# A patch transformer layer with top-1 experts: a per-image root moved from GpSimd to ScalarE, gate logits one reduction later, a chunk's loads reordered

## The reference

```
h    = patches @ W.T + b + pos                      # (32, 1024, 64)
p    = softmax((h@Wq.T+bq) @ (h@Wk.T+bk).T / 8)     # with a mask where q or k starts with 0
h    = norm(h + (p @ (h@Wv.T+bv)) @ Wo.T + bo)
e    = argmax(h @ gate_w + gate_b)                  # 8 experts, probability prb = softmax(...)[e]
pos  = place of the token in its expert's queue; kept = pos < 5120
y    = relu(h @ w1[e] + b1[e]) @ w2[e] + b2[e]      # for kept tokens
h    = norm(h + nan_to_num(y * prb * kept))
norm(x) = (x - mean(x)) / sqrt(var(x) + 1e-5)
```

## Time and profile before

| | |
|---|---|
| median of 3 runs | 1057.18 us (1056.9 to 1058.4) |
| the profiled execution | 1059.39 us, its span in the trace 1057.6 us |
| TensorE's mean granted clock | 0.952 of full speed |
| busy, of the span | TensorE 90%, VectorE 80%, ScalarE 66%, GpSimd 65% |
| windows 8 to 29 | 28.27 and 28.7 us in turn |
| from the last score window's start to the end | 892.5 to 1057.6 us |

### The profile page before, as it was taken

One profiled execution on the slowest core, in us unless ns is written; L12 is line 12 of the kernel. 1 busy time (PEld: TensorE's weight loads), 2 busy tenths in 40 slices (PEclk: granted clock), 3 DMA queues, 4 the chain that ended last, 5 costly groups with the idle time before them and its releaser, 6 DMA issues.

```text
span 1057.6 us, 19702 instructions
## 1 busy us (share of the span) xinstructions
PE 952.4 (90%) x6046; PEld 530.8 (50%) x6046; DVE 846.5 (80%) x1709; ACT 697.7 (66%) x1192; POOL 691.5 (65%) x689
## 2 busy tenths in 40 slices
PE   3799999999999999999999999999999999856740
PEld 2355545555555555555555555555555555433420
DVE  3667787788888888899989988888889897575561
ACT  2355655777777777777777777777777766545650
POOL 0015444456777777777777777777777777777775
PEclk9699999999999999999999999999999999967775
DMA  3332224334435243334443343424343333035300
GB/s 91 81 77 58 58 59 112 99 85 105 106 79 130 75 110 103 94 96 108 103 107 96 104 109 93 121 68 121 94 104 97 97 93 103 21 106 145 103 22 10
DMA packets 72503, 96.25 MB, mean 91 GB/s; under 512 B 15923, under 2 KB 52230, under 8 KB 72398
## 3 DMA queue, kind: packets, MB, share of 16 engines
q1 hardware_dynamic: 55566, 77.87, 29.7%
q0 software_dynamic: 16832, 17.11, 5.4%
HBM read 43.68 MB, written 18.11 MB: 58 GB/s over the span
## 4 chain that ended last, share of the span: by engine, by line
PE 57%; DVE 23%; ACT 9%; issue 7%; DMA 2%; POOL 1%; SPq 1%; POOLq 0%; DVEq 0%; ACTq 0%
PE p_u L590 14%; DVE mx L1003 8%; PE p_st L568 7%; PE p_misc L605 6%; PE p_misc L513 6%; PE p_misc L669 5%; PE p_misc L536 4%; PE p_sm L550 3%; ACT uu L793 3%; PE p_misc L653 3%; DVE qk L988 2%; ACT qk L759 2%; PE p_st L572 2%; PE p_sm L669 2%; ACT b_h L835 2%
## 5 line engine op out<-in xcount | busy, mean ns | idle before, releaser
L1376 POOL DMA_INDIRECT out<-b_o,b_ix x270 | 295.4, 1094 | 93.4 <-issue 69.3
L1363 POOL DMA_INDIRECT slots<-rows,idx x256 | 252.2, 985 | 146.8 <-issue 87.0
L1003 DVE TENSOR_REDUCE mx<-p_sm 128x1 f32<-128x1024 f32 x252 | 307.1, 1218 | 38.6 <-PE p_sm L552 35.6
L788 ACT ACTIVATE pT<-p_st 128x1024 f32<-128x1024 f32 x256 | 261.8, 1023 | 93.4 <-PE p_st L574 80.5
L590 PE MATMUL p_u<-pT,vv 128*64 128x512 f32 x1024 | 253.7, 605 | 0.0
L568 PE MATMUL p_st<-hi,hx 64*128 64x512 f32 x256 | 127.3, 497 | 5.1 <-ACT pT L788 4.0
L570 PE MATMUL p_st<-hx,hi 64*128 64x512 f32 x256 | 127.3, 497 | 0.0
L590 PEld LDWEIGHTS p_u<-pT,vv 128*64 128x64 f32 x1024 | 61.5, 136 | 105.2 <-issue 94.9
L550 PE MATMUL p_sm<-kh,hi 64*128 64x512 f32 x252 | 103.1, 409 | 10.3 <-DVE mx L1003 6.7
L568 PEld LDWEIGHTS p_st<-hi,hx 64*128 64x128 f32 x256 | 46.9, 183 | 127.3 <-issue 99.7
L835 ACT ACTIVATE b_h<-p_misc,b_w 128x256 f32<-128x256 f32 x244 | 95.6, 475 | 11.5 <-PE p_misc L653 5.2
(11 more groups left out here) (194 smaller groups left out, 1908.5 us busy)
## 6 DMA issues: line engine op xcount, KB each, us to landing
b_w<-in_w SPq DMA_DIRECT2D x136, 193.5 KB
hx<-hi SPq DMA_DIRECT2D x64, 256.0 KB, 3.6
b_in<-slots SPq DMA_DIRECT2D x136, 66.0 KB
lx<-lo SPq DMA_DIRECT2D x32, 256.0 KB
xt<-in_x SPq DMA_DIRECT2D x32, 196.0 KB
out<-b_o,b_ix POOLq DMA_INDIRECT x270
kh<-kh SPq DMA_DIRECT2D x32, 128.0 KB, 2.2
lx<-lo SPq DMA_DIRECT2D x32, 128.0 KB
```

Source lines behind the costliest of these rows:

```text
L788: act.activation(pT[k % 4][:, :], flat(p_st), ACT.Exp).then_inc(exp_done, 1)
L1003: dve.tensor_reduce(mx[:, p, at:at + 1], flat(max_place(n, j)), AX.X, ALU.max).then_inc(max_done, 1)
L1363: pool.indirect_dma_start(slots, bass.IndirectOffsetOnAxis(ap=idx[:, p, j:j + 1], axis=0), rows[:, p, j, :], None, bounds_check=SLOTS - 1, ...
L1376: pool.indirect_dma_start(out_rows, bass.IndirectOffsetOnAxis(ap=b_ix[:, o, j:j + 1], axis=0), b_o[:, o, j, :], None, bounds_check=T - 1, ...
```

## The change

Four edits:

- The root of the norm behind the attention is made on ScalarE for every image (`norm_root`: logarithm into sd, exponent into rstd), at place 5, or at place 6 in windows with a chunk. The two GpSimd steps and tile ve are gone. `norm_rows` on GpSimd and `gate_logits` on VectorE wait for the same semaphore as before, rstd_ready.
- `gate_logits` moves to place 6 in windows with a chunk, behind `row_max` of that place.
- HIK goes from 2 to 1, and the call of `qk_high` from ahead of the place's exponent to the end of the place.
- `load_chunk` asks for a chunk's rows first, then its four weights; inside the windows each weight waits for one more score of the window (places 4 to 7).

```
-HIK = 2
+HIK = 1
...
-        PS = 2
+        PS = 1
...
                     sp.dma_start(b_in[:, r, u, t, :], unit_rows(at[k])).then_inc(c_loaded[r], 16)
-
+                for k in range(2 * PAIRS):
+                    v, u = k // 2, k % 2
+                    if c < INSIDE:
+
+                        sp.wait_ge(st_done, NT * (HOST[c] - 1) + NT // 2 + 1 + k)
                     sp.dma_start(b_w[:, r, v, u, :], w[bass.ds(e[k], 1), :, :].rearrange("a k f -> (a k) f"))\
                         .then_inc(c_loaded[r], 16)
...
-            def last_deviation():
-                act.wait_ge(vs_ready, NB)
-                act.activation(sd[:, :], vs[:, :], ACT.Ln, bias=b_eps[:, 0:1], scale=1.0 / D).then_inc(last_sd_ready, 1)
-                act.wait_ge(last_sd_ready, 1)
+            def norm_root(n):
+                act.wait_ge(vs_ready, n + 1)
+                if n >= 1:
+                    act.wait_ge(tail_g, GS * (n - 1) + 1)
+                    act.wait_ge(pool_step, n)
+                act.activation(sd[:, :], vs[:, :], ACT.Ln, bias=b_eps[:, 0:1], scale=1.0 / D).then_inc(sd_ready, 1)
+                act.wait_ge(sd_ready, n + 1)
                 act.activation(rstd[:, :], sd[:, :], ACT.Exp, scale=-0.5).then_inc(rstd_ready, 1)
...
-                    if k == HIK and has(2):
-                        qk_high(b + 2)
...
-                    if k == 5 and b == NB:
-                        last_deviation()
+                    if k == (5 if m is None else 6) and has(-1):
+                        norm_root(b - 1)
                     if m is not None and k in (4, 5):
                         rectify(m, k - 4)
...
                     if k in (3, 6) and has(1):
                         v_copy(b + 1, q, k // 6)
+                    if k == HIK and has(2):
+                        qk_high(b + 2)
...
                         if j == 5 and b == NB:
                             dve.wait_ge(rstd_ready, NB)
-                        if j == 5:
+                        if j == (5 if m is None else 6):
                             gate_logits(b - 1)
...
-            def norm_root(n):
-
-                wait_apart(pool, vs_ready, n + 1)
-                counted(n, 1, pool.tensor_scalar(ve[:, :], vs[:, :], 1.0 / D, EPS, ALU.mult, ALU.add))
-                pool.tensor_tensor(rstd[:, :], ve[:, :], c_half[:, :], ALU.pow).then_inc(rstd_ready, 1)
-
             def norm_rows(n, p):
```

More of the change, by code:

```diff
@@ L113, in build @@
         w_t, c_centre, w_v, w_oT, w_g, w_bv, w_bl = views(c_deep, DEEP)
-        c_half = sb("c_half", [P, NT])
         c_neg = sb("c_neg", [P, QT])
@@ L151, in build @@
         vs = sb("vs", [P, NT])
-        ve = sb("ve", [P, NT])
         rstd = sb("rstd", [P, NT])
@@ L336, in build @@
         pool_step = sem("pool_step")
-        last_sd_ready = sem("last_sd_ready")
+        sd_ready = sem("sd_ready")
         last_rows_ready = sem("last_rows_ready")
@@ L979, in _ @@
             dve.memset(ones16[:, :], 1.0)
-            dve.memset(c_half[:, :], -0.5)
             dve.memset(b_eps[:, :], EPS)
@@ L1350, in norm_rows @@
                 pool.tensor_tensor(rows[:, p, :, 0:D], uc[:, :, 0:D], per_token(rstd[:, :], D), ALU.mult)
-                counted(n, 2, pool.tensor_scalar(rows[:, p, :, D + 1], rows[:, p, :, D + 1], float(2 * S), None,
+                counted(n, 1, pool.tensor_scalar(rows[:, p, :, D + 1], rows[:, p, :, D + 1], float(2 * S), None,
                                                  ALU.add))
@@ L1360, in scatter @@
                     else:
-                        wait_apart(pool, pool_step, PS * n + 2)
+                        wait_apart(pool, pool_step, PS * n + 1)
                 for j in tiles:
@@ L1394, in step @@
                     scatter(b - 2, par, range(4, NT))
-                    norm_root(b - 1)
                     spread_out(done, range(5))
```

## The result

| | before | after |
|---|---|---|
| median | 1058.07 us (14 runs, 1055.97 to 1059.77) | 1060.76 us (14 runs, 1059.87 to 1062.66) |
| after / before | | 1.003, 95% interval 1.0022 to 1.0038 |
| the profiled execution, its span | 1059.39, 1057.6 us | 1059.89, 1058.1 us |
| windows 11 to 29, without / with a table | 28.27 / 28.70 us | 28.19 / 29.03 us |
| windows 1 to 5, summed | 118.88 us | 120.03 us |

(The runs of before in this table were made together with those of after. Windows 8 and 10 of after take 29.3 us.) The forecast was 1054.1 us and faster; the kernel is 2.7 us slower than before, outside the range. The two profiled executions differ by 0.5 us only.

What follows compares the result with a forecast made beforehand. TensorE, busy 90% of the span, was taken as the bound. The terms -5.7 + 2.2 + 1.0 - 0.6 gave -3.1 us, from a median of 1057.18 to 1054.1 us; range 1052.0 to 1056.5.

Steps and rivals of the forecast that it cites:

- What bounds: TensorE, busy 90% of the span, sets the windows; key steps that start late by x lengthen the window by x.
- Gate logits one place later: Place 7: TensorE's 0.43 us wait for VectorE's reduction of place 6 goes in thirteen windows, -5.7 us.
- The block: VectorE's first logits operation, released with GpSimd's rows step, is held its whole length: 0.1 at each of 22 starts, +2.2 us.
- The cover of 0.86 and 0.60: Waits of VectorE's shift and key steps that absorb lateness: 0.86 without a table; with one, 0.34 + 0.69 less 0.43.
- The full length or the early rows' 0.22?: Price of VectorE's logits meeting GpSimd's rows: the whole length of rows (chosen), or 0.22 us as in early windows.
- The block outgrows its cover: Rival, chance 0.1: at key steps of 22 windows, GpSimd's rows take 1.48; 1065.9 us, slower from 0.34 lost per start.
- The wait goes and comes back: Rival, 0.18: VectorE loses 0.25 per start, or ScalarE's pair delays the value copy and down product; no gain, 1057 us.
- The block costs nothing: Rival, chance 0.22: lg loses only 0.22 us, far below the cover of 0.86; 1050.9 us.
- The root on ScalarE: Logarithm and exponent behind place 6's exponent, 0.54 us long; down product starts some 0.5 later, counted as nothing.
- Early windows: Windows b = 1 to 5, key steps without cover: 0.2 us left in each, +1.0 us.
- SP's loads: Chunk loads reordered, last weights requested at about 633 instead of 626.76: nothing, 0.5 us either way.
- The end: From window 31 on, GpSimd without the root starts the last scatters at 943.1 instead of 943.77: -0.6 us.

Runs made afterwards that it cites:

- h3: Kernel before, root still on GpSimd, with gate logits at place 6 in windows with a chunk and GpSimd's rows step waiting behind VectorE's pri: 1047.32 us, ratio 0.9902.
- h1: Changed kernel with one wait more, GpSimd's rows step behind VectorE's step pri: 1047.36 us, ratio 0.9891 to the kernel before.

## Why the prediction was wrong

**What bounds.** Right for the kernel before. The rule that key steps which start late by x make the window longer by x held as well: 0.34 lost per start is TensorE's new wait of 0.34 ahead of L607. What fell is the size of x.

**Gate logits one place later, -5.7.** The waits went, all thirteen. The mechanism was right, as h3 shows: with nothing held up this move is worth 11 us, more than the 5.7. Its windows 16 to 24 take 28.33 us with a table and 27.81 without one in the regular ones, 0.37 and 0.46 less than before; the first is what the term has, and for the second it had nothing. In the changed kernel the 0.43 of every second window was outweighed by 0.34 at each of the 22 starts. Where the 0.46 of the other windows comes from was not looked into.

**The block, +2.2: this term failed, by its size in table windows.** Its mechanism was right. The forecast for windows without a table was 0.94 later at place 7, 1.04 with the 0.1 for lg slipping in first. From the key steps to place 7 it was 21.29 and is 22.34 us, that is 1.05 later. For table windows the forecast was 0.7 late at the shift, with the reason that place 6 is still being reduced when the root comes. From the key steps to place 7 it was 21.69 and is 22.98, that is 1.29 later, and 1.17 at the shift, since the one-hot step got 0.12 back. In window 20 VectorE reached lg 0.18 behind the root. GpSimd was not waiting for the root, as the prediction supposed, but was still at its fifth output transfer, and lg was held from 605.10, during that transfer, to the end of rows. The working had taken the gate steps against ScalarE's root alone, and never laid GpSimd's own row of transfers beside it. The cover of 0.86 and 0.60 was right: 1.05 less 0.11 and 0.86 leaves 0.08, 1.17 less 0.60 leaves 0.57, together 0.65 for two windows where 0.68 was measured. By the sum two windows were to take 56.97 - 0.43 + 0.2 = 56.74 us; they take 57.22, that is 0.68 lost in two windows, or 0.34 per start instead of 0.1. The difference, 22 x 0.24 = 5.3, is nearly all of the 5.8 us between -3.1 and +2.7.

**The full length or the early rows' 0.22?** The full length was chosen, from the earlier trace rows, against the early rows, and rightly, with 0.81 and 1.30 lost. The two were never different prices: in the earlier trace rows too lg ended 0.08 behind rows, and lost less only because rows was 0.68 on its way. In window 21 of the changed kernel lb ended 0.09 behind rows, and mx beside rows keeps its 1.22. What holds the step was not shown, and the order of the recorded starts does not decide it: lg in window 20 started 0.37 ahead of rows and was held, lg in window 21 started 0.13 ahead and kept its 0.23.

**The rivals.** "The block outgrows its cover" (0.1) is what happened, in its place and at its own point of decision. For 0.34 lost per start its working gave +2.2 us, and +2.7 was measured. Key steps right behind acc and windows of 28.6 on average (57.22 / 2) were its signs. The way there was wrong, and that the point of decision fits so well is in part luck: it had GpSimd's rows slowed to 1.48, for which it gave 1065.9, while rows kept its 1.06 and lg began too early. "The wait goes and comes back" (0.18) named the wait's return by a loss per start, took it at 0.25 and stopped at no change. "The block costs nothing" is refuted by the 29.9 us in lg and lb. A reduction beside rows does keep its length (mx, 1.22 or 1.23 us in all of 245 cases), but in the changed kernel lg or lb met rows too.

**The root on ScalarE, 0.** Right: the pair stands behind the exponent of place 6, from 604.39 to 604.92 in window 20, 0.53 long, and h1 with it is no slower than h3 without it.

**Early windows, +1.0.** Right: 1.15, four by 0.19 to 0.21 and the table window by 0.35.

**SP's loads, 0.** Right: 0.9991 and 0.9995 alone, with 1.000 in both intervals.

**The end, -0.6.** From the start of the shift of window 31 to the end after takes 162.7 us and before 165.1, that is 2.4 less in these two traces. The loads-only kernel, whose time is that of before, takes 163.8, so that 1.3 of the 2.4 can be chance; the term is not settled. Windows 7 and 30 are 0.3 shorter each, window 6 0.4 longer. (The granted clock in the trace of before is full until about 920 us and not until 940: it is 0.74 and 0.57 in the two stretches of 10 us behind 920.)

## What to carry to other kernels

A wait of the bounding engine is worth its length only if the engine it waits for has that much to spare (0.43 went in every second window here, and 0.34 came at each of 22 starts); add up the second engine's own loop, waits left out, before counting a removed wait as a gain. Idle time that stands beside an instruction in both traces, as the 0.81 ahead of L559 and L557, is no loss of the change, whatever releaser is named there. Where VectorE steps such as lg and lb (0.22 us, up to 1.53 when held) and a GpSimd step such as rows (1.04 to 1.09 us) are released by the same event, place the long one by hand beside reductions, which kept their lengths here (mx 1.22, lm and pm 0.22); one semaphore wait on GpSimd took the changed kernel from 1.003 to 0.989 of the time before, on one kind of chip. And lay the third engine's queue beside the step: what it does just ahead of the meeting counts as well (lg was held from 0.37 ahead of rows, during GpSimd's output transfer).

## What the runs showed of the hardware

In the sixteen traces lg, lb, ld or pri met GpSimd's rows step 273 times and was lengthened, and each time it ended 0.07 to 0.10 us behind rows. In 123 more meetings lg had started 0.03 to 0.13 us ahead of rows and kept its 0.22 or 0.23. The row maximum beside rows took 1.22 or 1.23 us in all of 245 cases, and the small reductions lm (62 cases) and pm (38) took 0.22. A step of 0.17 us (t_x) took 1.30 or 1.31 us in the twelve windows in which it met GpSimd's uc in the kernel before, and ended with it; beside an indirect transfer, at 168.05, it kept its 0.17.

VectorE was also held before GpSimd's operation had begun by the records: lg by 0.37 us, and pri in the logits-only run by 0.67, both from within GpSimd's preceding indirect transfer. In the six traces with GpSimd's root and no added wait, where the root had long been ready and rows followed a transfer at once, all of 129 steps that started up to 0.30 us behind the start of that transfer kept their length, and all of 48 that started 0.31 us behind it or later were held to the end of rows. Where the root came during the transfer, as in window 21 of the changed kernel, lg started 0.02 behind the root and kept its 0.23. So in these traces the hold did not begin with the recorded start of rows; with the root there, it began for steps from 0.31 us into the transfer ahead on. For a sum: pri was held from 0.67 us ahead of rows and took 1.83 us instead of 0.23, beside rows of 1.07. That the transfer itself holds the steps is not likely, since lb of the logits-only run lay at 0.81 in a transfer that another one followed, and kept its 0.22.

The kernel before differed by 7% between chips (1058 against 1131 and 1133 us), and the changed kernel took 1.003 of its time on the chip of the result and 1.122 on chip 9. A ratio needs the kernel before on the same chip, and a second chip before it is believed.
